# Two graph layers on one core: results kept in PSUM, key products in two halves around a table load, key sums straight from the split weights

## The reference

```python
def _L0_gnn_ref(x, adj, Wq_w, Wq_b, Wk_w, Wk_b, Wv_w, Wv_b):
    query = jnp.einsum('bnd,od->bno', x, Wq_w) + Wq_b
    keyt = jnp.einsum('bnd,od->bno', x, Wk_w) + Wk_b
    value = jnp.einsum('bnd,od->bno', x, Wv_w) + Wv_b
    weight = jnp.einsum('bqd,bkd->bqk', query, keyt)
    weight = adj * jnp.exp(weight)
    weight = weight / jnp.sum(weight, axis=2, keepdims=True)
    return jnp.einsum('bqk,bkd->bqd', weight, value)

def _L1_gnn_ref(x, adj, W):
    deg = jnp.sum(adj, axis=-1, keepdims=True)
    agg = jnp.einsum('bij,bjf->bif', adj, x) / jnp.maximum(deg, EPS)
    out = jnp.einsum('bnf,of->bno', jnp.concatenate([x, agg], axis=2), W)
    return jax.nn.relu(out)

h = jnp.maximum(_layernorm(x, axis=-1), 0.0)
x = x + _L0_gnn_ref(h, adj, ...)
h = jnp.maximum(_layernorm(x, axis=-1), 0.0)
x = x + _L1_gnn_ref(h, adj, L1_gnn_W)
```

## Time and profile before

| what | us |
|---|---|
| median of 3 runs | 1933.32 |
| lowest, highest | 1931.07, 1945.87 |
| the profiled execution | 1942.48 |
| its span | 1940.4 |
| TensorE busy in it (8956 matmuls) | 1892.7 |
| VectorE, GpSimd, ScalarE busy | 1579.6, 1103.0, 862.4 |

### The profile page before, as it was taken

How to read it: one execution, slowest core, us unless ns; L and a number is a source line. 1 busy time by engine, 2 the same in 40 slices (tenths; PEclk the granted TensorE clock), 3 DMA queues, 4 the chain that set the end, 5 groups by cost and what they waited for, 6 DMA issues and landing times.

```text
span 1940.4 us, 29261 instructions
## 1 busy us (share of the span) xinstructions
PE 1892.7 (98%) x8956; PEld 1576.8 (81%) x8956; DVE 1579.6 (81%) x2649; ACT 862.4 (44%) x1453; POOL 1103.0 (57%) x1066
## 2 busy tenths in 40 slices
PE   8899999999999999999999999999999999999997
PEld 5778888888888888888788888888888888887885
DVE  6887888888788888888878888887888878888776
ACT  4344444444444445443445443444444454434442
POOL 4665565565565565655655655655655656546552
PEclk9999999999999999999999999999999999999999
DMA  6456656566656566555566555566555665555632
GB/s 222 148 189 212 210 181 196 188 203 207 210 178 190 198 205 204 192 198 173 189 208 219 188 194 184 191 211 211 179 191 194 204 203 194 197 173 184 211 125 87
DMA packets 190881, 370.69 MB, mean 191 GB/s; under 512 B 17936, under 2 KB 115216, under 8 KB 182672
## 3 DMA queue, kind: packets, MB, share of 16 engines
q1 hardware_dynamic: 190864, 370.48, 57.2%
HBM read 266.60 MB, written 103.81 MB: 191 GB/s over the span
## 4 chain that ended last, share of the span: by engine, by line
PE 49%; DVE 19%; DMA 17%; issue 8%; SPq 4%; POOL 2%; ACT 1%; DVEq 1%; POOLq 0%; ACTq 0%
PE bank L518 16%; PE bank L520 16%; PE bank L519 16%; DMA turned_store<-blocks 8%; DMA n_l<-t_store 8%; DVE y L1223 3%; SPq L263 3%; DVE x L1235 3%; DVE stats L1091 2%; DVE x L1227 2%; DVE g_full L1213 2%; DVE deg L1112 1%; DVE mean_sum L1096 1%; DVE blocks L1073 1%; DVE sums L1252 1%
## 5 line engine op out<-in xcount | busy, mean ns | idle before, releaser
L403 POOL TENSOR_TENSOR hT_l<-turned,hT_h 128x512 fp32r<-128x512 f32 x122 | 181.9, 1517 | 264.0 <-ACT hT_h L824 263.9
L242 POOL TENSOR_TENSOR w_l<-w,w_h 128x512 fp32r<-128x512 f32 x62 | 80.3, 1295 | 307.5 <-ACT w_h L857 307.5
L1073 DVE STREAM_TRANSPOSE blocks<-h 128x512 f32<-128x512 f32 x252 | 163.3, 685 | 110.3 <-DMA turned_store<-blocks 110.3
L518 PE MATMUL bank<-hT_h,n_h 128*128 128x512 f32 x512 | 200.9, 392 | 3.9 <-DVE hT_l L1164 2.8
L519 PE MATMUL bank<-hT_l,n_h 128*128 128x512 f32 x512 | 200.2, 391 | 0.0
L520 PE MATMUL bank<-hT_h,n_l 128*128 128x512 f32 x512 | 200.2, 391 | 0.0
L518 PE MATMUL bank<-wv_h,hT_h 128*128 128x512 f32 x512 | 199.6, 390 | 0.0
L519 PE MATMUL bank<-wv_l,hT_h 128*128 128x512 f32 x512 | 199.5, 390 | 0.0
L520 PE MATMUL bank<-wv_h,hT_l 128*128 128x512 f32 x512 | 199.3, 389 | 0.0
L399 POOL TENSOR_TENSOR xb<-x_in,bv_b 128x512 f32<-128x512 f32 x128 | 165.9, 1301 | 43.5 <-DVE x L1235 39.3
L843 ACT ACTIVATE kz_h<-bank,kp_bias 128x512 fp32r<-128x512 f32 x128 | 83.6, 675 | 207.5 <-PE bank L520 207.5
(11 more groups left out here) (152 smaller groups left out, 5394.9 us busy)
## 6 DMA issues: line engine op xcount, KB each, us to landing
turned_store<-blocks SPq DMA_DIRECT2D x126, 512.0 KB, 4.5
turned<-turned_store SPq DMA_DIRECT2D x504, 128.0 KB, 2.9
x_in<-x SPq DMA_DIRECT2D x32, 1024.0 KB, 5.3
n_h<-t_store SPq DMA_DIRECT2D x31, 1024.0 KB, 6.3
n_l<-t_store SPq DMA_DIRECT2D x31, 1024.0 KB, 8.3
out<-x SPq DMA_DIRECT2D x124, 256.0 KB, 2.0
n_h<-n_store SPq DMA_DIRECT2D x60, 512.0 KB, 4.6
n_l<-n_store SPq DMA_DIRECT2D x60, 512.0 KB, 5.9
```

What stands on the lines that cost most here:

```text
L242: engine.tensor_tensor(w_l[:, g], w[:, g], w_h[:, g].bitcast(F32), ALU.subtract).then_inc(w_split, 1)
L403: pool.tensor_tensor(by_blocks(hT_l, t), turned_tile(t), by_blocks(hT_h, t).bitcast(F32), ALU.subtract).then_inc(hT_split, 1)
L518: pe.matmul(dst, lh, rh, start=first, stop=False, skip_group_check=more)
L1073: nc.vector.transpose(blocks[:, :, :, t % NT, :].rearrange("p j c b -> p c j b"), h[:, t, :].rearrange("p (c j b) -> p c j b", c=DT, b=Q)) ...
```

## The change

What is changed, in the order in which a step meets it:

- The key products are made in halves: `kp(i, dt, half)` takes two of the four terms. All four banks get their first half, then all four their second. After the first half SyncE loads T1 (512 KB for each of `n_h` and `n_l`), at the very start of the step's queue; T2 is loaded where both were loaded, behind `move_g`. TensorE waits for the halves apart.
- VectorE does the degrees and `turn_g(j, 0)` first and the four `low_kp` then; ScalarE does the first two norms ahead of `high_kp(i, 0)`.
- `exp` writes in place in PSUM, both graphs one after the other; `weigh` reads PSUM and writes `w`. `v(i, 2)` and `v(i, 3)` wait for `w_done`.
- The additions in `split_w`, `high_sum` and `low_sum` are gone. `sum_weights` sums over both key tiles of `w_h` and of `w_l`, with four matmuls of 512 columns.
- z is summed in the PSUM bank of product 1 and split from there; y is written to the bank that `az` held, which is free only at `x2_done`.
- In the first step the second weight matrix is loaded earlier, n is stored later, T2's and T4's splits come earlier. In the final step ScalarE copies product 0 and VectorE sums z before the degrees, and GpSimd splits the adjacency before A22. `combine_s4` of the final pair moves behind z.

```diff
@@ split_w
             engine.tensor_tensor(w_l[:, g], w[:, g], w_h[:, g].bitcast(F32), ALU.subtract).then_inc(w_split, 1)
-            engine.wait_ge(w_split, G * i + g + 1)
-            engine.tensor_tensor(w[:, g, 0, :], w[:, g, 0, :], w[:, g, 1, :], ALU.add).then_inc(w_summed, 1)
@@ SyncE
-            def load_t(i):
-                sp.wait_ge(kp_psum, DT * (i + 1))
-                sp.dma_start(n_h[:, :, :].bitcast(F32), t_d[0]).then_inc(t_loaded, 16)
-                sp.dma_start(n_l[:, :, :].bitcast(F32), t_d[1]).then_inc(t_loaded, 16)
+            def load_t(k):
+
+                half = slice(2 * k, 2 * k + 2)
+                sp.dma_start(n_h[:, half, :].bitcast(F32), t_d[0, :, half, :]).then_inc(t_loaded[k], 16)
+                sp.dma_start(n_l[:, half, :].bitcast(F32), t_d[1, :, half, :]).then_inc(t_loaded[k], 16)
...
             def step(i):
                 j = i - 1
+                if is_first(i):
+                    sp.wait_ge(n_stored, 32)
+                    sp.wait_ge(t_stored, 64)
+                sp.wait_ge(kp_half, i + 1)
+                load_t(0)
                 sp.wait_ge(xb_done, T * (i + 1))
                 load_x(i + 1)
                 move_g(j)
...
-                load_t(i)
+                sp.wait_ge(kp_psum, DT * (i + 1))
+                load_t(1)
@@ SyncE, GpSimd and ScalarE, first step
+            sp.wait_ge(setup_psum, DT)
+            sp.wait_ge(parts_done, 2 * DT + 1)
+            sp.dma_start(x1[:, :, :], w1_t[0:dim].rearrange("(t p) o -> p t o", p=P)).then_inc(wh_loaded, 16)
...
+                low_mix(T2)
                 for t in range(NT):
                     low_hT(1, t)
-                low_mix(T2)
+                low_mix(T4)
                 low_at(0)
@@ TensorE
+            def kp(i, dt, half):
+
                 cols = slice(dt * P, (dt + 1) * P)
...
+                kp(i, 0, 0)
+                kp(i, 1, 0)
                 if not is_first(i):
-                    pe.wait_ge(y_done, T * (i - 1))
-                kp(i, 2)
+                    pe.wait_ge(x2_done, T * (i - 1))
+                kp(i, 2, 0)
                 pe.wait_ge(sum_inv_done, i)
-                kp(i, 3)
+                kp(i, 3, 0)
+                if not is_first(i):
+                    pe.wait_ge(n_loaded[1], 32 * (i - 1))
+                for dt in range(DT):
+                    kp(i, dt, 1)
...
                 if t >= 2:
-                    pe.wait_ge(exp_done, NT * (G * i + t - 1))
+                    pe.wait_ge(w_done, G * i + t - 1)
...
+                for n, part in enumerate((w_h, w_l)):
+                    for c in range(NT):
+                        mm = pe.matmul(every, all_ones, part[:, :, c, :], start=(n == 0 and c == 0),
+                                       stop=(n == 1 and c == NT - 1))
...
-                pe.wait_ge(t_loaded, 32 * i)
+                pe.wait_ge(t_loaded[0], 32 * (j + 1))
                 pe.wait_ge(v_split, T * i + 2)
                 strassen(j, 2, 0)
                 strassen(j, 2, 1)
                 pe.wait_ge(part_split, 7 * j + S2)
+                pe.wait_ge(t_loaded[1], 32 * (j + 1))
@@ ScalarE
+                    keys = bank[SCORE_BANK[g]][:, kt * nodes:(kt + 1) * nodes]
+                    nc.scalar.activation(keys, keys, ACT.Exp, bias=key_bias[:, NT * g + kt:NT * g + kt + 1]).then_inc(exp_done, 1)
@@ VectorE
-                nc.vector.tensor_tensor(w[:, g], w[:, g], adjT[:, NT * g:NT * (g + 1), :], ALU.mult).then_inc(w_done, 1)
+                nc.vector.tensor_tensor(w[:, g], bank[SCORE_BANK[g]][:, :].rearrange("p (t n) -> p t n", n=nodes),
+                                        adjT[:, NT * g:NT * (g + 1), :], ALU.mult).then_inc(w_done, 1)
...
-                nc.vector.tensor_tensor(z_sum[r], bank[Y_BANK[r]][:, :], z_sum[r], ALU.add).then_inc(z_summed, 1)
+                nc.vector.tensor_tensor(bank[Y_BANK[r]][:, :], bank[Y_BANK[r]][:, :], p0_copy[r], ALU.add).then_inc(z_summed, 1)
...
-                nc.vector.scalar_tensor_tensor(out=y[:, :], in0=bank[az_bank][:, :],
+                nc.vector.scalar_tensor_tensor(out=bank[az_bank][:, :], in0=bank[az_bank][:, :],
                                                scalar=deg_inv[:, t:t + 1], in1=(u2, ha1)[g][r],
                                                op0=ALU.mult, op1=ALU.add).then_inc(y_done, 1)
                 dve.wait_ge(y_done, T * j + t + 1)
-                nc.vector.scalar_tensor_tensor(out=place[:, t, :], in0=y[:, :], scalar=0.0, in1=place[:, t, :],
+                nc.vector.scalar_tensor_tensor(out=place[:, t, :], in0=bank[az_bank][:, :], scalar=0.0, in1=place[:, t, :],
```

More of the change, by code:

```diff
@@ L563, in first_kp @@
                 for dt in range(DT):
-                    kp(0, dt)
+                    for half in range(2):
+                        kp(0, dt, half)
             def all_kp(i):
```

181 lines of the change are left out of this document (76 added, 105 removed).

## The result

The changed kernel takes 1919.01 us (median of 7 runs, 1917.18 to 1920.49) against 1933.32 for the kernel before (1931.07 to 1945.87): a ratio of 0.9908, 95% interval 0.989 to 0.9926. That is 0.9% less. The runs of before spread over 14.8 us, those of after over 3.3. The profiled execution of after took 1919.01 us, just its median, where that of before stood 9.2 us above its own.

What follows compares the result with a forecast made beforehand. TensorE was taken as the bound, busy 1892.7 of 1940.4 us. Loop -12.2, start -9.4 and end -5.5 sum to -27.1 us off the profiled 1942.48: 1915.4, rounded to 1916, range 1905 to 1932.

Steps and rivals of the forecast that it cites:

- Loop, -12.2: 29 loop steps: waits and slow restarts go (-27.3 us), added key-sum matmuls cost +13.6, late S2 +1.5.
- 0.05 per step: Product 3 in each loop step: allowance for S2 still arriving slightly late, +1.5 us in all.
- x and z: VectorE's tail: x falls from 1143 to about 692 ns with a PSUM operand, 1.8 us less per step, helping S2.
- Start, -9.4: Ahead of step 2: earlier T2 chain takes 6.8 us off step 1, its head wait and slow restart 2.6.
- Step 31, ±0: Step 31 unchanged within 0.1 us: +0.47 for the matmuls, offset by a late z of the same size going.
- End, -5.5: Final step: z made first removes TensorE's 5.8 us lateness and slow restart; S2 may be 1 us late instead.
- The 9.2 us: Profiled execution's excess over the median, read mainly as table waits differing between executions, so not subtracted again.
- rival B: The 9.2 us are a general offset of profiled executions, so runs fall to 1906 us; chance 0.12.
- A: S2 takes the table wait's place, 0.2 to 0.3 us late in each step: 7.3 us, 1923; chance 0.24.
- D: Table wait stays in part as T2's load shares its window: at most 0.3 us per step, 1924; chance 0.06.
- C: T1's early load delays x and the first store; TensorE waits about 1.5 us per step: 1958 us; chance 0.05.
- PSUM as a source: Counter-argument: a PSUM source's 62 extra cycles cost each x 65 ns, making S2 late, +7.5 us at worst.

Runs made afterwards that it cites:

- e2: Kernel before with halved key products, early T1 load, two waits and new step-head order only; y, z, exp and key sums as before: 1938.02 us, ratio 0.9967 to before.
- e9: The changed kernel run again unaltered, on the third chip: 1921.39 us, ratio 0.9890 to before there.
- e12: Changed kernel with the old order of ScalarE, VectorE and GpSimd in the final step, PSUM results kept, fourth chip: 1922.12 us, ratio 1.0018 to before there.
- e1: Changed kernel with T1's load put back beside T2's, the two waits kept, second chip: 1915.62 us, ratio 0.9849 to before there.
- e4: Changed kernel with y back in an SBUF tile, so x has two SBUF operands, third chip: 1927.21 us, ratio 0.9921 to before there.
- e5: Changed kernel without the two key-sum matmuls on w's low parts, only to measure their price, third chip: 1903.09 us, ratio 0.9799 to before there.
- e7: Changed kernel with n's stores and both moves ahead of the store of T1's parts in the first step, fourth chip: 1916.54 us, ratio 0.9985 to before there.
- e3: Changed kernel with the old key sums (additions, split, two matmuls) restored, third chip: 1906.81 us, ratio 0.9818 to before there.
- e1b: Changed kernel with T1's load beside T2's and one wait for both ahead of product 2, second chip: 1924.99 us, ratio 0.9899 to before there.
- e13: Changed kernel with T1's load issued between x and the first store of turned blocks, fourth chip: 1934.20 us, ratio 1.0083 to before there.

## Why the prediction was right, and where it wasn't

I predicted 1916 us and a range of 1905 to 1932; measured are 1919.01. The answer "within 1%" had 0.58. That it is on this side of 1% is luck: the start gave 5.3 us less than I took, and with them the time would be 1913.7, just over 1% below before. The measured interval, 0.989 to 0.9926, has the border in it.

**Loop, -12.2.** Measured -12.2. Both halves of the sum are confirmed apart: without the two matmuls the floor is 57.96, with them 58.40, so they cost 0.44 per step (I took 0.47); and the table wait is gone. So the exact hit is two small misses that cancel, 0.8 us less for the matmuls and 0.8 more for the rest. The 0.05 per step that I left for S2 came out as 0.08, but for another reason than given: not a chain short by a fixed 0.2 us but a few steps whose store lands late.

**x and z.** x at 692 ns, as expected. What this was for I had only half right: I needed it for S2, and it is at least as much what keeps `low_kp` in time for the scores, which I had called unchanged ("the four `low_kp` end where the last one ended before"). With the old tail (e2) they are 0.5 us late.

**Start, -9.4.** Measured -4.1, and this is the step that failed. I took 6.8 us off step 1 by pulling the chain behind ScalarE's 9.31 us wait forward, and 2.6 more at its head. The first is right but for its size: the wait shrank to 1.55 us, and step 1 went from 66.46 to 61.35, 5.1 us (66.5 to 66.8 in the three profiles with before's start, 60.4 to 61.4 in after, e9, e12, e1, e4 and e5). The second is the term that failed: TensorE waits 3.1 us for h's low parts instead of 2.79, and from the first key product to step 1's it is 41.3 us where it was 40.7. The other profiles say the same: 39.3 to 41.5 with before's start, 40.5 to 41.3 with after's. The remaining 0.5 us lies ahead of the first key product, and this start differs by up to 2 us between profiles. I had counted the new order of the queue as free. SyncE now stands for T1's split ahead of the moves; e7 took that wait away, and the time went into VectorE's low parts beside GpSimd. The 5.12 us for w's low parts are a second suspect that e3 doesn't bear out. Why the head gained nothing is thus known in part only.

The restart behind this wait is slow, and I had counted on its going. These are rows of TensorE's windows (stretch, its length, busy time and matmuls, the granted clock as a share of 2.4 GHz, DMA share, GB/s), first of before, then of after, last of e1, where the wait at this place is 2.6 us:

```profile
68.80:84.00 15.20, 15.12 (x60) 0.89 0.30 105
84.00:98.00 14.00, 10.44 (x63) 0.88 0.56 187
```
```profile
69.90:84.00 14.10, 14.06 (x50) 0.78 0.74 270
84.00:98.00 14.00, 14.00 (x86) 1.00 0.60 200
```
```profile
69.90:84.00 14.10, 13.16 (x60) 1.00 0.51 189
```

A mean of 0.78 or 0.89 means that the clock was at 1.2 GHz for a part of the time. Over the two stretches before and after lose about as much by it (0.11 x 15.2 + 0.12 x 14.0 = 3.4 us, and 0.22 x 14.1 = 3.1), so it explains no difference between them. Nor does it set the step's length: e1 ran at the full clock, and its step 1 takes 61.17 us. What the 2.9 us are that step 1 takes over a step of the loop I did not part. Step 2 beginning at 131.28, not 126, is the miss in one number.

**Step 31, ±0.** +0.4. The added matmuls are paid there too, and the cover I had named wasn't one: the late operand at 1900.53 of before was `g_full`, not z, and it is as late in after.

**End, -5.5.** -7.4. I held 1 us back for a late S2, which wasn't late, and counted the slow restart short: the 18 matmuls from the waiting one on took 1924.51 - 1918.75 = 5.8 us in before and 1901.27 - 1897.14 = 4.1 in after.

**The 9.2 us.** I read them as table waits that differ between executions. The changed kernel's profile, which has none, stands at its median, and its runs spread a quarter as far. Before's own second profile waits longer in total and takes longer. Against rival B (a general offset) speak all the others: of the twelve other profiled executions none stood more than 1.3 us above the median of its kernel. Before's two profiles stood 9.2 and 6.9 above theirs; whether that is chance, or profiling lengthens the waits for transfers, is open.

**The rivals.** A's mechanism, S2 late in each step, didn't come. D's didn't either; e1b shows how near it was. C was right that the early load makes the store late, and too high in price. I had written that 5 us lie between T1 and x; in after they are 2.83 us apart, because x goes out earlier too, once the tail is shorter. A few stores then land 2 to 3 us late, as C says, but most steps absorb it. e13 shows the full price, 0.5 us per step and not 1.5.

**What the change is worth** depends on the chip. After itself wasn't run on the fourth. From e12 and e7, 1922.12 less 8.3 for the end or 1916.54 less 1.9 for the start, it would take 1914 to 1915, an estimate. That would be some 0.2 to 0.3% below before's 1918.97 there, where it is 1.1% on the third.

**PSUM as a source.** The rule that gives a PSUM source 62 cycles more (the Trainium skill, "VectorE: DVE Perf Modes", section "The TRN2 errata — SBUF-src ops pay a fixed extra latency per instruction") isn't seen here: x takes 692 ns from PSUM and took 692 from SBUF with GpSimd idle. I had written that forms with a PSUM operand have no row of their own in before; for x that is so, but z's low part had one:

```profile
L1070 DVE TENSOR_TENSOR kz_l<-bank,kz_h 128x512 fp32r<-128x512 f32 x64 | 44.2, 691 | 25.9 <-ACT kz_h L813 25.8
```

It settles both points ahead of any run: 691 ns from PSUM against 1283 from SBUF, in one kernel. Writing y to PSUM costs 759 ns where it was 751 in e4, which still writes it to SBUF.

## What to carry to other kernels

When a transfer is late, first split the wait for it, so that each half is awaited where it is used; moving its issue forward is the second step, and it has to be checked against what it then stands ahead of in the same queue. Before work is moved to the bound engine to relieve others, ask whether one of the others is still waited for once the rest of the change is in: here it was not in the loop, and the two matmuls cost 0.44 us in each step. And a chain that is pulled forward can land beside another engine's work on the same memory, and lose there what it gained.

## What I had not expected

- The kernel before takes 1919 us on one chip and 1942 on two others (median each), while after took 1921 on one of the two and, by an estimate, 1914 to 1915 on the first. The kernel that waits for transfers differs by 24 us, the one that hardly waits by some 7. That the waits make the difference isn't shown.
- With 3.26 us or more between two loads of 1 MB the store behind them took at most 6.0 us, in every step of four kernels from the third on; with 2.83 us it took up to 8.4, though in one kernel only once more than 7.5.
- Two VectorE instructions with SBUF operands took 1.29 us with no GpSimd instruction beside them, and 5.22 us when they started 1.2 us earlier and met two.
